# Destination rows of a graph kernel: one fp32 product, or three two-byte products of three parts

## What is computed

```
def _gatv2(x, src, dst, edge_attr, Wl, bl, Wr, br, We, att, bo):
    xl = x @ Wl.T + bl
    xr = x @ Wr.T + br
    e = edge_attr @ We.T
    m = xl[src] + xr[dst] + e
    score = jnp.where(m > 0, m, NEG_SLOPE * m) @ att
    smax = jax.ops.segment_max(score, dst, num_segments=N)
    smax = jnp.where(jnp.isfinite(smax), smax, 0.0)
    es = jnp.exp(score - smax[dst])
    denom = jax.ops.segment_sum(es, dst, num_segments=N)
    alpha = es / (denom[dst] + 1e-16)
    out = jax.ops.segment_sum(alpha[:, None] * xl[src], dst, num_segments=N)
    return out + bo
```

## Time and profile before

| | us |
|---|---|
| median of 3 runs | 15595.16 (15594.63 to 15600.81) |
| the profiled execution, its own time | 15726.75 |
| its span, first to last instruction | 15725.0 |
| PE busy | 7775.5 (49%) |
| PE weight loads busy | 6870.1 (44%) |
| DVE busy | 6482.9 (41%) |
| ACT busy | 3617.1 (23%) |
| POOL busy | 7853.4 (50%) |
| mean granted TensorE clock | 0.602 of 2.4 GHz |

### The profile page before, as it was taken

How to read it: one execution, slowest core, us unless ns; L and a number is a source line. 1 busy time by engine, 2 the same in 40 slices (tenths; PEclk the granted TensorE clock), 3 DMA queues, 4 the chain that set the end, 5 groups by cost and what they waited for, 6 DMA issues and landing times. The chain is left out here.

```text
span 15725.0 us, 179050 instructions
## 1 busy us (share of the span) xinstructions
PE 7775.5 (49%) x38719; PEld 6870.1 (44%) x38720; DVE 6482.9 (41%) x11706; ACT 3617.1 (23%) x4964; POOL 7853.4 (50%) x8083
## 2 busy tenths in 40 slices
PE   0555555545555554445455454444444645454442
PEld 0545554535444454444444434444444334444442
DVE  3344444444444445233333334444444424343444
ACT  0222222212222221222222212222222122222220
POOL 3455555525555552555555415555554045555551
PEclk9566666656666666555555555555555555555665
DMA  2333333333333332222222223333333233333331
GB/s 68 78 81 79 79 78 76 79 62 77 78 75 77 77 76 47 49 45 47 45 46 44 44 97 85 76 76 75 75 76 76 68 96 83 82 83 83 83 75 22
DMA packets 1913054, 1107.36 MB, mean 70 GB/s; under 512 B 1548686, under 2 KB 1593762, under 8 KB 1911874
## 3 DMA queue, kind: packets, MB, share of 16 engines
q1 hardware_dynamic: 1654786, 718.42, 18.5%
q0 software_dynamic: 257568, 382.66, 12.3%
HBM read 1003.35 MB, written 96.52 MB: 70 GB/s over the span
## 5 line engine op out<-in xcount | busy, mean ns | idle before, releaser
L973 POOL DMA_INDIRECT ds_gat<-table_d,ds_idx x1568 | 1504.7, 960 | 1618.9 <-issue 864.1
L973 POOL DMA_INDIRECT es_gat<-table_e,es_idx x1568 | 1533.2, 978 | 1344.1 <-issue 700.1
L973 POOL DMA_INDIRECT bs_gat<-table_b,bs_idx x1568 | 1531.1, 976 | 1255.1 <-DMA bs_idx<-idx_d 742.4
L973 POOL DMA_INDIRECT as_gat<-table_a,as_idx x1568 | 1539.1, 982 | 1211.6 <-DMA as_idx<-in_srcT 710.2
L973 POOL DMA_INDIRECT cs_gat<-table_c,cs_idx x1568 | 1527.6, 974 | 1177.1 <-DMA cs_idx<-idx_d 586.0
L1238 PE MATMUL es_psA<-es_ahot,es_wtd 128*68 128x128 f32 x3136 | 641.0, 385 | 499.6 <-ACT es_psA L998 351.3
L1238 PE MATMUL cs_psA<-cs_ahot,cs_wtd 128*68 128x128 f32 x3136 | 677.5, 400 | 334.9 <-ACT cs_psA L998 233.4
L1223 PE MATMUL cs_psM<-cs_dst,cs_hot 128*128 128x4 f32 x3136 | 607.5, 324 | 454.6 <-DMA cs_dst<-dst_c 370.4
L1223 PEld LDWEIGHTS cs_psM<-cs_dst,cs_hot 128*128 128x128 f32 x3136 | 596.8, 291 | 518.5 <-DMA cs_dst<-dst_c 268.7
L1238 PEld LDWEIGHTS es_psA<-es_ahot,es_wtd 128*68 128x68 f32 x3136 | 572.2, 212 | 523.7 <-issue 523.1
L1238 PE MATMUL bs_psA<-bs_ahot,bs_wtd 128*65 128x128 f32 x3136 | 632.8, 369 | 311.2 <-issue 269.7
(11 more groups left out here) (717 smaller groups left out, 16569.5 us busy)
## 6 DMA issues: line engine op xcount, KB each, us to landing
ds_dst<-dst_d SPq DMA_DIRECT2D x1568, 34.0 KB
as_rank<-rel_d SPq DMA_DIRECT2D x196, 256.0 KB
as_dst<-dst_a SPq DMA_DIRECT2D x1568, 32.0 KB
as_ea<-in_eaT SPq DMA_DIRECT2D x196, 256.0 KB
bs_rank<-rel_d SPq DMA_DIRECT2D x196, 256.0 KB
bs_dst<-dst_b SPq DMA_DIRECT2D x1568, 32.0 KB
bs_ea<-in_eaT SPq DMA_DIRECT2D x196, 256.0 KB
cs_rank<-rel_d SPq DMA_DIRECT2D x196, 256.0 KB
```

Source lines behind the costliest of these rows:

```text
L973: g_.indirect_dma_start(gat[s][:, j, :], None, table, bass.IndirectOffsetOnAxis(ap=idxS[s][:, j:j + 1].bitcast(U32), axis=0)).then_inc(got ...
```

## The change

The destination rows are stored as three bf16 parts whose sum is the fp32 number: a row of 3 x 64 two-byte numbers (384 bytes where there were 256; 24 for 16 in layer c, 408 for 272 in d).

- In `tables`, DVE makes the parts once it is through with its copies to `st`: in three pieces of 17 windows, for each piece cast, subtract, cast, subtract, cast, each waiting for the one before. Then SP writes three pieces of `dstP` instead of five of `dstF`, after all pieces of the table.
- In `stream`, `dsts` and `hot` are bf16, and `expand` has three products for each tile, with the same stationary one-hot, that add up in PSUM.

```
-            d["dst"] = dram(f"dst_{spec['name']}", [RANKS + P, spec["dst"]])
+            d["dst"] = dram(f"dst_{spec['name']}", [RANKS + P, 3 * spec["dst"]], BF16)
...
+        dstP = sb("dstP", [P, KR + 1, 3, dc], BF16)
...
+        HALF = [0, 17, 34, KR + 1]
...
-                kept = [0, 10, 20, 30, 40, KR + 1]
                 def put_dst(q):
-                    sp.wait_ge(tookA, min(kept[q + 1], KR))
-                    if q == 4:
-                        sp.wait_ge(xch, 2)
-                    sp.dma_start(dstR[:, kept[q]:kept[q + 1], :], dstF[:, kept[q]:kept[q + 1], :]).then_inc(kept_d, 16)
+                    lo, hi = HALF[q], HALF[q + 1]
+                    sp.wait_ge(parted, q + 1)
+                    sp.dma_start(dstR[:, lo:hi, :], dstP[:, lo:hi, :, :].rearrange("p w t c -> p w (t c)")).then_inc(kept_d, 16)
...
+                v.wait_ge(xch, 2)
+                n = 0
+                for q in range(3):
+                    lo, hi = HALF[q], HALF[q + 1]
+                    v.wait_ge(tookA, min(hi, KR))
+                    for part in range(3):
+                        v.tensor_copy(dstP[:, lo:hi, part, :], dstF[:, lo:hi, :]).then_inc(pieces, 1)
+                        n += 1
+                        v.wait_ge(pieces, n)
+                        if part < 2:
+                            v.tensor_tensor(dstF[:, lo:hi, :], dstF[:, lo:hi, :], dstP[:, lo:hi, part, :], ALU.subtract).then_inc(pieces, 1)
+                            n += 1
+                            v.wait_ge(pieces, n)
+                    v.sem_inc(parted, 1)
...
-        dsts = [sb(f"dst{s}", [P, GROUP, dc]) for s in range(4)]
-        hot = [sb(f"hot{s}", [P, GE]) for s in range(2)]
+        dsts = [sb(f"dst{s}", [P, GROUP, 3 * dc], BF16) for s in range(4)]
+        hot = [sb(f"hot{s}", [P, GE], BF16) for s in range(2)]
...
-                        last = pe.matmul(psM[s % 2][:, j * DW:j * DW + dc], hot[s % 2][:, j * P:(j + 1) * P], dsts[s % 4][:, j, :],
-                                         start=i > 1, stop=True, skip_group_check=i <= 1)
+                        for part in range(3):
+                            last = pe.matmul(psM[s % 2][:, j * DW:j * DW + dc], hot[s % 2][:, j * P:(j + 1) * P],
+                                             dsts[s % 4][:, j, part * dc:(part + 1) * dc],
+                                             start=part == 0 and i > 1, stop=part == 2, skip_group_check=i <= 1)
```

16 lines of the change are left out of this document (7 added, 9 removed).

## The result

The changed kernel took 15921.55 us (median of 4 runs, 15893.91 to 15961.33) beside 15597.99 us before (4 runs, 15594.63 to 15648.42): ratio 1.0202, 95% interval 1.0168 to 1.0236, 324 us slower. The prediction was 15657 us with a range up to 15785. Slower was right, the size was not: the tables cost about what was worked out for them, and the streams, which were to stay as they were, took most of the rest.

What follows compares the result with a forecast made beforehand. Bound: POOL's gather run, SP's rest of a group and the indices' landing; in layer d DVE with stalls, not PE. Terms 54.6 + 11 + 8 - 12 = +62 us on 15595 gave 15657 us, range 15565 to 15785.

Steps and rivals of the forecast that it cites:

- 54.6 + 11 = 66: Tables, on the path: DVE's casts and subtractions add 54.6 us over five layers, the larger last transfers 11 us.
- upper bound for a piece, 6.5 us: Tables: DVE's five steps on 17 windows if casts cost what subtractions do; 5.0 us was taken.
- Layer a's cover: Layer a's tables: two of three pieces hide while ACT fills `dstF`; 5.0 us stays, 15 without cover.
- The expansion was to take 2.6 us: Streams: a group's 24 two-byte pairs on PE at 0.107 us each, 0.9 us less than before.
- rival 1: Streams, layer d: PE's gain reaches the path, 176 us faster, 15481 us; chance 0.14.
- In a stall PE's instructions come 0.7 us apart ... Nothing on the path: Streams, slow stretches during POOL's gathers: added instructions cost PE some 2 us in 28, DVE and SP equally held; 0.
- Wider rows: Streams: indices land later behind wider destination rows each time POOL starts anew; 8 us taken, 8 to 31 possible.
- PE's gain at the streams' ends: End of each stream, no POOL running: PE saves 0.9 us on the last four or so expansions; -12 us.
- 2: Streams, layer d: half of rival 1's gain or less, as DVE takes over; -65 us, 15592 us; chance 0.13.
- 3: Streams: wider rows delay indices 0.3 us at each of POOL's restarts; 118 us, 15775 us; chance 0.13.
- 4: Streams: two-byte pairs no cheaper than fp32, SP waits for `made`; 670 us, 16320 us; chance 0.05.

Runs made afterwards that it cites:

- two_products: Changed kernel with only the first two parts' products, 4 PE instructions for a tile; tables and transfers unchanged: 1.0012 of the kernel before.
- narrow_parts: Changed kernel with the second and third parts' products one column wide, still 6 PE instructions for a tile: 1.0146 of the kernel before.
- rounded_rows: Kernel before with two-byte destination rows written by ACT, no parts, and one product, 2 PE instructions for a tile: 0.9815 of the kernel before.
- one_product: Changed kernel with only the first part's product, 2 PE instructions for a tile; tables and transfers unchanged: 0.9929 of the kernel before.
- split6_before: Kernel before with POOL waiting ahead of a group only for the first six gathers of the group before, next to no pause: 0.9939 with stalls.
- paced2_before: Kernel before with POOL waiting ahead of each group for the gathers of the group before the last: 1.0030 of the kernel before.
- short_loads: one_product with only the first part of each destination row loaded, a third of the changed kernel's bytes: 0.9923 of the kernel before.
- after_third: The changed kernel run again, unedited, beside other runs on another chip: 1.0212 of the kernel before.
- the paced kernels: Kernel before and changed kernel, each with POOL waiting ahead of a group until the previous group's gathers have landed: 0.9047 and 0.9109 of the kernel before.
- paced_before: Kernel before with POOL waiting ahead of each group's eight gathers until those of the group before have landed: 0.9047 of the kernel before.

## Why the prediction came out where it did

**The tables: right in place, 13 us short.** Forecast 54.6 + 11 = 66, measured 79. The step that was off is the cast: taken from `pr_relB` as 0.73 us for 1088 columns, it takes 1.29, as much as a subtraction. The 0.16 us of fixed cost in that estimate is a term that no run shows; the cast of 2048 columns took 0.60 ns for a column and these take 1.18, into an output whose rows of 64 stand 192 apart. Which property of the cast makes the difference no run tells. The prediction's own upper bound for a piece, 6.5 us, is the right value.

```profile
L761 DVE CAST bt_dstP<-bt_dstF x9: 1275/1286/1287, 3436.0 to 3454.7; 128x1088 bf16<-128x1088 f32 x9
L765 DVE TENSOR_TENSOR bt_dstF<-bt_dstF,bt_dstP x6: 1291/1292/1293, 3437.3 to 3453.4; 128x1088 f32<-128x1088 f32 x6
```

With 9 x 0.56 = 5.0 us more in b and e, 5.4 in d and 1.7 in a, the steps come to 72, which leaves 7 for the transfers (11 forecast). That share was put in the wrong layers, though. From DVE's last step to the stream's first instruction it takes 5.4 us in b, less than the 6.5 from ACT's last copy before; in layer c it takes 13.8 where it took 6.9, so that c, whose rows are the shortest, pays more than the other four together; 1 us was forecast for it.

```profile
6321.81 0.48 DVE L1019 MEMSET cs_zero<- 128x512 f32 x1 [6.81 <-PEq L587]
...
6427.45 0.22 DVE L761 CAST ct_dstP<-ct_dstF 128x68 bf16<-128x68 f32 x1
...
6441.43 0.48 DVE L1031 MEMSET cs_zero<- 128x512 f32 x1 [13.76 <-DMA agg_a<-am_merged,bS]
```

The first line is the kernel before, where ACT's last copy ended at 6314.88. Layer a's cover held: 6.2 us there.

**PE's time: too dear, and harmless.** The expansion was to take 2.6 us. In layer d, at a granted clock of 0.50 of full speed, that is the 1.2 GHz level, 24 loads take 1.38 us, 58 ns each; a fp32 load of 128 columns took 218 ns.

```profile
9991.20 1.38 PEld L1236 LDWEIGHTS ds_psM<-ds_dst,ds_hot 128*128 128x128 bf16 x24 [1.56 <-issue]
```

The same 3 us by stretch: length, busy time and instructions of PE, PEld and DVE, then the granted clock, the share of DMA and GB/s.

```profile
9990.00:9993.00 3.00, 1.52 (x24) 1.38 (x24) 0.32 (x2) 0.50 0.49 103
```

The Trainium skill (TensorE: Matmul & The Clock Gate, Weight-path perf modes) says that full-width weights of another type than fp32 load about twice as fast; by that rule the estimate was 1.5 us, and the trace agrees (1.4 to 1.5; 58 ns are about half of the 107 reckoned without it). PE's saving was 2 us a group, twice the forecast, and rival 1 would have made layer d shorter by it. It did not, and the added count isn't the reason: in two_products, with the count of before and 0.92 us for 3.49, layer d is at 14.76 for 14.82.

**The failed step: "In a stall PE's instructions come 0.7 us apart ... Nothing on the path".** It put the loss at some 2 us of PE's in 28 and held it to be covered because DVE and SP are held up as well. What the runs show in its place: two more instructions for each tile at almost equal PE time are the 1.3% between two_products and narrow_parts, a third pair of full width is 2% (two_products and the changed kernel), and SP's wait for PE rises from 35 to 336 us in layer a and from 591 to 1030 in d.

The reading: in a stall PE gets so many instructions and no more, 17 in 12 us if all are 0.7 us apart, whatever they are, and PE needs some 80 of its own for a group of layer a (16 for edge attributes, 32 for rows, 32 to collect), now 96. A stall used to carry PE 0.21 of a group and now carries it 0.18; nothing makes up for that where PE has no slack.

The count of steps by itself doesn't give the time. Layer a holds some 119 more products 0.7 us apart than before and is 81 us longer, d some 143 for 71 us, but c and e 128 and 147 for -7 and +10 us, and with the loads counted too the steps 0.7 us apart go from 489 to 792 in a and from 37 to 662 in c. What differs is PE's slack. When SP asks for a group's ranks, so many groups, that one included, lie unexpanded, of five that the waits allow: in c 1.9 before and 3.2 after, in e 2.0 and 3.3, in a 3.2 and 3.8, in d 4.0 and 4.0; rounded_rows has 2.1 in a and 1.9 in d. These counts are shown. That the missing slack turns the steps into time is a reading; it fits a, c, d and e, and it fits one_product, where only d became shorter. Layer b, 3.4 and 3.8, doesn't fit in this pair of profiles: 108 more such products for 6 us. But its stream before, 13.87 us for a group, is longer than in the three other kernels with four instructions and stalls (13.58 to 13.72 in split6_before, two_products and paced2_before), so that may be the one execution's.

**Behind it stood a misread row.** The prediction took SP's waits for `made` to be 1.3 us in a and 35.8 in d, the rows that name PE. But in layer d, from 9340 to 12200 us, SP's queue before also had this, at the same line, where it waits for `made` and reads the windows, and an index load can't be what it waits for:

```profile
SPq L944 <- DMA as_idx<-in_srcT: 540.3, 72, 14.3
```

After, in d from 9480 to 12400 us and in a from 500 to 3220 us:

```profile
SPq L956 <- DMA as_idx<-in_srcT: 1012.9, 77, 17.2
...
SPq L956 <- remote: 334.3, 39, 17.9
```

Before, a had 33.2 us of the last kind. With two PE instructions for a tile there is no such row in d, in one_product and short_loads as in rounded_rows, so it was PE that SP waited for. DVE's "remote" waits in the earlier trace rows were read as stalls in which the semaphore had long been given. For those at L1037 (300.4 us), which take PE's sums, this is wrong in part: in half of the 40 that are longer than 3 us a product of PE's had ended less than 0.2 us before. With 540 us read as "SP is late at the row transfers of layer d", the claim that PE isn't late could not have stood.

**Wider rows: nothing against it.** 8 us taken; between one_product and short_loads, with three times the bytes, lie 0.0006 of the time, which is within the noise. That was measured with two PE instructions for a tile, not with six.

**PE's gain at the streams' ends: wrong in sign.** -12 taken. Between POOL's last gather of a layer and its first of the next the four gaps grew by 24, 12, 45 and 24 us, and the tables explain 19, 10, 24 and 20 of it. The largest rest is at the end of layer c: from POOL's last gather to the merge it took 56.5 us before and takes 76.8 (75.5 in after_third, 51.3 and 51.8 in the paced kernels), so there the consumers lag further behind POOL when it stops. The gain that was forecast is seen only with two instructions: in one_product that stretch is shorter in all but c.

**Rivals.** 1 and 2 did not come, 3 did not (short_loads), 4 was ruled out by the loads (58 ns for 218). That the change would be slower was forecast and came out, but only the tables' 79 us of it for the reason given. The case that did come was on no list: more instructions, not slower ones.

## What to carry to other kernels

Count instructions per engine as well as their time, above all for a change that splits one into several: where a trace has stretches in which an engine's instructions come at a fixed distance, added ones can cost time on an engine without slack, however short they are. Read an impossible releaser as an unexplained wait and size it before calling an engine idle. And when one engine's long run goes with slow stretches of others, try to break the run, but only where the profile shows such stretches: a pause of 2 us in each group brought 9.5% with stalls, one of 1.2 us cost 7% without.

## What the hardware showed

- On four chips instructions of PE and of SP's queue come 0.7 or 1.4 us apart for 10 us and more while POOL issues runs of up to 24 indirect gathers; DVE and ACT show long waits there, but no such spacing. With a pause of about 2 us after each eight, when all have landed, PE's slow steps all but vanish (products 127 to 8 in layer a) and SP's fall by a third over the five layers (9294 to 5955), for 0.9047 of the time; a mere bound on gathers under way brings little or nothing (0.9939, 1.0030). A fifth chip had none (117 such steps of SP's, 1568 gathers in one run) and ran the same kernel in 12255 us instead of 15596 to 15763.
- A pair of PE instructions for each tile, a load and a one-column product of zeros, cost 2.1 to 2.5% of the kernel: 7840 pairs for 325 to 389 us, 41 to 50 ns each, on an engine that is busy half the time, on chips with stalls. The pair lengthens PE's expansion of a group by 0.8 us, so this is not the price of the count alone.
- A two-byte load of 128 columns took 58 ns at the 1.2 GHz level (granted clock 0.50), a fp32 load 218.
- A cast of 1088 columns from fp32 to bf16 into every third row of 64 took 1.29 us, one of 2048 columns in a row 1.23.
- Faster than both kernels where stalls are: paced_before (0.9047, nothing left out, not run on the chip without stalls) and rounded_rows (0.9815, rows rounded to two bytes).
